# An edge loop of a graph network: 20 groups of 18 blocks instead of 15 groups of 24, and one wait and one signal of TensorE per up to three one-hot tiles

## The reference, cut to what matters

```python
h = jnp.maximum(_layernorm(x, axis=-1), 0.0)
row, col = (edge_index[0], edge_index[1])
out = jnp.concatenate([x[row], edge_attr], axis=1)   # x is h here: a row is gathered for each edge
h1 = out @ W1a + b1a                                 # 212500 x 128
h1 = jax.nn.relu(_bn(h1, g1a, be1a))                 # mean and variance over all edges
out = h1 @ W2a + b2a
out = jax.ops.segment_sum(out, col, num_segments=x.shape[0])
```

## Time and profile before

| what | before |
|---|---|
| median of 3 runs | 5176.9 us |
| the profiled execution's own time | 5175.57 us |
| its span, first to last instruction | 5173.8 us |
| mean granted TensorE clock | 0.761 of full |
| gathers of the edge loop (L1210) | 1604, in 401 blocks |
| one-hot tiles (L1268) | 1470, in 15 groups |

### The profile page before, as it was taken

How to read it: one execution, slowest core, us unless ns; L and a number is a source line. 1 busy time by engine, 2 the same in 40 slices (tenths; PEclk the granted TensorE clock), 3 DMA queues, 4 the chain that set the end, 5 groups by cost and what they waited for, 6 DMA issues and landing times. The chain is left out here.

```text
span 5173.8 us, 34611 instructions
## 1 busy us (share of the span) xinstructions
PE 2846.9 (55%) x9306; PEld 1329.6 (26%) x9408; DVE 2941.6 (57%) x4622; ACT 1084.8 (21%) x1623; POOL 3485.5 (67%) x3690
## 2 busy tenths in 40 slices
PE   2012232323232323232359898988888899577676
PEld 2001111111111111111123333333333333255455
DVE  6224444444454545456446566666666666399994
ACT  8000000000000000001221111111111111188883
POOL 6667777777777777777677777777777777611112
PEclk8556666666666666665569999999999999788887
DMA  9723333333333333332344444444444444299992
GB/s 348 248 59 90 81 90 81 90 81 90 81 90 82 89 83 88 84 86 66 76 106 107 105 112 112 105 107 112 112 109 103 112 112 108 68 383 422 417 414 88
DMA packets 507862, 698.10 MB, mean 135 GB/s; under 512 B 357862, under 2 KB 376519, under 8 KB 462256
## 3 DMA queue, kind: packets, MB, share of 16 engines
q1 hardware_dynamic: 364353, 562.73, 33.6%
q0 software_dynamic: 117152, 126.61, 11.8%
q10 hardware_dynamic: 26166, 6.56, 0.6%
HBM read 356.30 MB, written 339.24 MB: 134 GB/s over the span
## 5 line engine op out<-in xcount | busy, mean ns | idle before, releaser
L837 POOL DMA_INDIRECT hid<-send_table,node_sums x1664 | 1570.3, 944 | 507.1 <-issue 507.1
L1210 POOL DMA_INDIRECT shared<-norm_table,node_sums x1604 | 1513.8, 944 | 489.0 <-issue 473.1
L873 PE MATMUL ps_msg<-hidden,w_quarters 128*128 128x512 f32 x832 | 617.4, 910 | 1469.0 <-ACT hidden L902 1469.0
L1494 DVE TENSOR_SCALAR one_hot<-ps_mask 128x512 bf16<-128x512 bf16 x1470 | 574.1, 418 | 636.4 <-PE ps_mask L1268 568.6
L941 DVE STREAM_TRANSPOSE send_t<-hid 128x1024 f32<-128x1024 f32 x104 | 131.0, 1260 | 1045.7 <-DMA hid<-send_table,node_sums 1045.7
L873 PEld LDWEIGHTS ps_msg<-hidden,w_quarters 128*128 128x128 f32 x832 | 238.2, 301 | 1847.6 <-ACT hidden L902 1534.9
L1268 PE MATMUL ps_mask<-one_hot,node_sums 128*64 128x512 bf16 x1470 | 598.5, 407 | 20.8 <-issue 12.1
L1267 PE MATMUL ps_mask<-one_hot,ring 128*128 128x512 bf16 x1368 | 538.8, 394 | 0.0
L902 ACT ACTIVATE hidden<-joined 128x1024 f32<-128x1024 f32 x104 | 109.9, 1056 | 1969.3 <-DVE joined L945 1969.3
L1333 ACT COPY shared<-ps_back 128x512 f32<-128x512 f32 x401 | 234.8, 585 | 1326.6 <-PE ps_back L1235 1326.2
L1527 DVE TENSOR_TENSOR_SCAN ring<-ps_mask,ring 128x1024 f32<-128x1024 f32 x207 | 486.4, 2350 | 44.9 <-PE ps_mask L1311 21.6
(11 more groups left out here) (227 smaller groups left out, 2778.9 us busy)
## 6 DMA issues: line engine op xcount, KB each, us to landing
hid_edges<-shared SPq DMA_DIRECT2D x104, 1024.0 KB, 8.8
hid_edges<-ring SPq DMA_DIRECT2D x99, 1024.0 KB, 4.6
ring<-hid_edges SPq DMA_DIRECT2D x99, 1024.0 KB, 10.8
recv_edges<-node_sums SPq DMA_DIRECT2D x52, 1024.0 KB, 5.9
hid<-recv_edges SPq DMA_DIRECT2D x416, 128.0 KB
recv_edges<-hid SPq DMA_DIRECT2D x416, 128.0 KB, 2.3
shared<-in_edge_attr_dram SPq DMA_DIRECT2D x415, 128.0 KB, 5.4
hid<-send_table,node_sums POOLq DMA_INDIRECT x1664
```

The lines of the kernel that those rows point to most:

```text
L837: pool.indirect_dma_start(out=send_in[:, s, j * C:(j + 1) * C], out_offset=None, in_=send_table, in_offset=bass.IndirectOffsetOnAxis(ap=sr ...
L873: mm = nc.tensor.matmul(ps_msg[k % M][:, d, :], w2_quarters[:, b, d, :], hidden[:, s % 2, b, :], start=b == 0, stop=b == BANDS - 1)
L1210: pool.indirect_dma_start(out=pairs[:, s, j, 0:C], out_offset=None, in_=norm_table, in_offset=bass.IndirectOffsetOnAxis(ap=src_cols[:, b / ...
L1494: nc.vector.tensor_scalar(one_hot[:, n % OH, :], hot_of, float(t + 1), None, ALU.is_equal).then_inc(hot_made, 1)
```

## The change

The number of blocks in a group goes from 24 to 18, and the number of groups from 15 to 20, so that 20 of the 416 blocks are made by products instead of 15; both cover the 360 blocks from 36 to 395. The 98 tiles of a group are spread over 17 blocks instead of 23, five or six in each. The ring of one-hot tiles stays at eight.

Besides, the tiles of a block are taken in batches of up to BATCH = 3. TensorE waits for `hot_made` once per batch, for the batch's last tile, and raises `hot_used` once, at the batch's last product. `hot_used` now counts batches, and all that wait for it (DVE before it overwrites a slot of the ring, ACT before it takes the sums, SP, POOL and DVE after the last group) ask for the number of the batch that holds the tile. A batch doesn't reach over the end of a block.

```diff
--- before.py
+++ after.py
@@ -1020,10 +1020,11 @@
             TILES = NI
             TC = SPLIT * C
             FIRST = U + 2 * NSTEP3
-            GROUP = 24
-            NPE = 15
+            GROUP = 18
+            NPE = 20
             OH = 8
-            assert FIRST + NPE * GROUP <= NBLK - HR * PER and TILES <= 5 * (GROUP - 1) and GROUP > U
+            BATCH = 3
+            assert FIRST + NPE * GROUP <= NBLK - HR * PER and TILES <= 7 * (GROUP - 1) and GROUP > U
             ring = tensor(s4, "ring", [P, max(HR * CHUNK, 2 * CHUNK + TILES * C)])
             hid = ring[:, 0:HR * CHUNK].rearrange("p (u f) -> p u f", u=HR)
             table_hm = ring[:, 2 * CHUNK:2 * CHUNK + TILES * C].bitcast(BF16).rearrange("p (t h c) -> p t h c", t=TILES, h=2)
@@ -1130,6 +1131,12 @@
 
                 return sum(len(tiles_of(i)) for i in range(k))
 
+            batch_of = []
+            for k in range(NBLK):
+                first = batch_of[-1] + 1 if batch_of else 0
+                batch_of.extend(first + i // BATCH for i in range(len(tiles_of(k))))
+            batches_to = [batch_of[TILES * g + TILES - 1] + 1 for g in range(NPE)]
+
             def gathers_of(k):
 
                 return len([i for i in range(k % U, k + 1, U) if not by_products(i)])
@@ -1176,7 +1183,7 @@
                 for q in range(2):
                     sp.wait_ge(hid_out[q], 16 * in_slot_before(q))
 
-                sp.wait_ge(hot_used, TILES * NPE)
+                sp.wait_ge(hot_used, batches_to[-1])
                 sp.dma_start(masks, same_sum.rearrange("(p c) -> p c", c=CO)).then_inc(masks_in, 16)
 
                 def load_hid(k, _):
@@ -1215,7 +1222,7 @@
 
 
                 pool.wait_ge(node_taken, NI_PAD)
-                pool.wait_ge(hot_used, TILES * NPE)
+                pool.wait_ge(hot_used, batches_to[-1])
                 pool.wait_ge(chunks_out, HR)
                 for i in range(NI):
                     needed = pool.value_load(chunks_needed[0:1, i:i + 1], min_val=1, max_val=CHUNKS)
@@ -1258,15 +1265,18 @@
                     k = r * U + s
                     g, _ = group_of(k)
                     n = hot_count(k)
-                    for t in tiles_of(k):
+                    end = n + len(tiles_of(k))
+                    for i, t in enumerate(tiles_of(k)):
                         if t == 0:
                             at_least(pe, last_made, NSTEP3)
                             at_least(pe, sums_taken, 2 * g)
-                        at_least(pe, hot_made, n + 1)
+                        if i % BATCH == 0:
+                            at_least(pe, hot_made, min(n + BATCH, end))
                         first, last = t == 0, t == TILES - 1
                         nc.tensor.matmul(acc_hm, table_hm[:, t, :, :].rearrange("p h c -> p (h c)"), one_hot[:, n % OH, :], start=first, stop=last)
                         mm = nc.tensor.matmul(acc_lo, table_lo[:, t, :], one_hot[:, n % OH, :], start=first, stop=last)
-                        mm.then_inc(hot_used, 1)
+                        if n + 1 == end or (i + 1) % BATCH == 0:
+                            mm.then_inc(hot_used, 1)
                         n += 1
 
                 def turn_node(r, s):
@@ -1333,7 +1343,7 @@
                         nc.scalar.copy(pairs_t[:, s % 2, :], ps_pairs[s % 2]).then_inc(copied, 1)
                         return
                     g, _ = group_of(k)
-                    at_least(act, hot_used, TILES * (g + 1))
+                    at_least(act, hot_used, batches_to[g])
                     nc.scalar.copy(sums_hm.rearrange("c (p j) -> c j p", j=J), acc_hm.rearrange("c (j p) -> c j p", j=J)).then_inc(sums_taken, 1)
                     nc.scalar.copy(pairs_t[0:C, s % 2, :].rearrange("c (p j) -> c j p", j=J),
                                    acc_lo.rearrange("c (j p) -> c j p", j=J)).then_inc(sums_taken, 1)
@@ -1429,7 +1439,7 @@
                     if k % PER == 0:
                         at_least(dve, hid_out[slot_of(c)], 16 * in_slot_before(c))
                         if c == HR - 1:
-                            at_least(dve, hot_used, TILES * NPE)
+                            at_least(dve, hot_used, batches_to[-1])
                     part = hid_part(k)
                     nc.vector.tensor_scalar(part, ps_hid[s % 2], vec[:, 0:1], None, ALU.add).then_inc(hid_made, 1)
                     at_least(dve, hid_made, k + 1)
@@ -1490,7 +1500,8 @@
                     for t in tiles_of(k):
                         if t == 0:
                             at_least(dve, own_turned, g + 1)
-                        at_least(dve, hot_used, n - OH + 1)
+                        if n >= OH:
+                            at_least(dve, hot_used, batch_of[n - OH] + 1)
                         nc.vector.tensor_scalar(one_hot[:, n % OH, :], hot_of, float(t + 1), None, ALU.is_equal).then_inc(hot_made, 1)
                         n += 1
```

## The result

The changed kernel takes 5478.3 us (median of 4 runs, 5477.7 to 5479.1) against 5176.8 for the kernel before in the same measurement: ratio 1.058, 95% interval 1.057 to 1.060. It is 301.5 us slower; 283 were forecast.

What follows compares the result with a forecast made beforehand. POOL's gathers were taken to bound the edge loop, TensorE close behind. 20 x (93.6 + 8.2), less about 5, gives 2031 us against 1720.6: +310, less 27 is +283 on 5176.9, so 5460 us; range 5285 to 5500.

Steps and rivals of the forecast that it cites:

- part 1: Edge loop, POOL: 20 gathers fewer take 25 us off, counting only where POOL sets the pace.
- part 2: Edge loop: with more tiles TensorE needs 93.6 us a group, above POOL's 84.9, and becomes the bound.
- part 3: Six-tile blocks after six-tile blocks: the late signal stalls TensorE's product 0.91 us, 8.2 us a group.
- part 4: TensorE's tiles: 1280 waits and 1280 signals fewer, taken to gain nothing, at most 20 us.
- part 5: End of edge loop: POOL runs eight blocks ahead, last tile to last gather 65 us instead of 93, 27 back.
- A: Edge loop: the bound passes to TensorE but DVE's lateness is covered, +119 us, 5296; chance 0.12.
- B: TensorE's tiles: weight loads slip under the preceding product, 0.44 us a tile, POOL bounds again, 5152; chance 0.06.
- C: TensorE in the edge loop: short stalls pull the clock down, adding 94 us, 5554; chance 0.06.
- D: Edge loop: no change, as slightly cheaper tiles let TensorE and the head start balance; chance 0.02.

Runs made afterwards that it cites:

- 5: Changed kernel with the low part's product made 128 columns wide: 5151.3 us, ratio 0.995 to the kernel before.
- 1: Changed kernel, groups of 18, with one wait and one signal per tile (BATCH = 1): 5307.5 us, ratio 1.026 to the kernel before.
- 3: Changed kernel with nine slots instead of eight in the ring of one-hot tiles: 5309.0 us, ratio 1.026 to the kernel before.
- 4: Changed kernel with `finish` and `aggregate` ahead of `make_hot` and `make_own` on DVE: 5270.1 us, ratio 1.018 to the kernel before.

## Why the prediction was right, point by point

- *Fewer gathers* (part 1). 25 us are worth what was said, but only where POOL sets the pace, as in 5; in the changed kernel they are lost.
- *The bound passes to TensorE* (part 2). The bill of 93.6 us a group without late signals gave 119 us over the kernel before; 131 were measured (1). The term that was mis-sized is the clock. The terms are those of the trace (0.656 a tile, 0.49, 0.86; at the border 2.75 us from the transposes to L1251, where 2.48 + 0.33 = 2.81 were reckoned), and a group whose clock stays up takes 93.3. The forecast held the clock at its upper level throughout; in 1 it falls at twelve borders, which is 12 x 1.55 = 19 us, and the bill was 0.3 a group too high, 5 or 6 us. In the changed kernel two falls cost 3 us.
- *The stall of the late signal* (part 3). Signals one by one, a ninth slot, or `finish` first each remove it with DVE's load unchanged (1, 3, 4). 0.91 us was reckoned for a six after a six. The trace has 1.337 - 0.493 = 0.844 and 0.07 for the late pair. One step was incomplete: I followed the sixth tile alone. In a six after a five, DVE's fourth, fifth and sixth tiles all hang on the first signal and are made one after another, so `finish` comes 3 x 0.33 later. That is 0.44 + 0.98 + 0.89 = 2.31 against a cover of 2.14, and the timeline has it (three one-hot tiles in one row from 3343.91, L1444 at 3344.91, the product 0.68 after the transposes):

```profile
3343.47 0.40 PE L1277 MATMUL ps_mask<-one_hot,node_sums 128*64 128x512 bf16 x1
...
3343.91 1.09 DVE L1505 TENSOR_SCALAR one_hot<-ps_mask 128x512 bf16<-128x512 bf16 x3 [1.93 <-PE ps_mask L1277]
...
3344.91 0.74 DVE L1444 TENSOR_SCALAR ring<-ps_back,vec 128x512 f32<-128x512 f32 x1
...
3345.12 0.66 PE L1242 MATMUL ps_back<-ident,shared 128*128 128x128 f32 x4
...
3345.80 0.67 PE L1252 MATMUL ps_back<-shared,w1a 128*128 128x512 f32 x1
```

  Four such blocks in each of 20 groups, at 0.19 + 0.07, make 21 us. With the 3 us of the clock, and less the 5 or 6 by which the bill was too high, that is the 18 us by which the forecast for first to last tile (2031) fell short of 2049.
- *Waits and signals gone* (part 4). Nothing, as taken: pairs with and without one are as far apart, and a group takes 93.3 us with a signal for each tile (1) and with few (3). The 16 ns from which the upper bound was worked out go with the product of 64 columns: with 128, both distances are 0.22 (5). The Trainium skill's 26.3 ns a signal (TensorE: Matmul & The Clock Gate, "The cost: per-tile semaphore tail") isn't seen: the trace disagrees, with products one after the other and not side by side.
- *The head start* (part 5). 65 us were reckoned from the last tile to the last gather, 64.9 are measured.
- *Rivals.* A (lateness covered) falls: the stalls are in the trace, and 1 and 3 take them away. B (the load slips under) falls as told, with waits and signals as its cause, but its sum came out: with the tile shortened by another means, 5151 were measured where it gave 5152. That is in part luck. B left the stalls at 8.2 us a group, while they grow as the tiles get shorter (1.43 us from transposes to product in 5, where it was 1.34); the expectation of 5 put the whole bill at 85, just level with POOL's 84.9. C falls: the clock was 1.00 over the loop, and the short stalls didn't pull it down. D falls with the time.

## What to carry to other kernels

A signal that is given once per batch frees the slots of a ring late. Here the engine that fills the ring (DVE) waited for that signal, and behind this wait stood other work (`finish`) that the engine that empties the ring (TensorE) needed in turn. Look for such a wait, and put the other work first or add a slot. Before moving work from a saturated queue to a neighbour, sum the neighbour's bill start to start: here a reserve of 13 us in 115 became a deficit of 9 in 85 when groups shrank by a quarter, because the 64 us of a group's tiles don't shrink with it. And where two products alternate in width, try the narrow one at full width.

## What wasn't expected of the hardware

Multiplying the low part with twice the columns made TensorE faster: 0.43 us a tile instead of 0.656, most likely because the load of a bf16 weight of 128 columns between products of 128 was hidden here and one of 64 was not. The other is the clock: with the same wait of 2.2 us at the borders, it fell at twelve of twenty in experiment 1 and at two of twenty in the changed kernel, which idles more in sum. With 1.2 us there, in experiment 4, it fell at none. What decides it stays open.
